# A 1-core transformer block: value products of the second batch moved from the setup into the lead of attention, and two operand stacks where there were three

## What is computed

```python
mod = jax.nn.silu(c) @ w_adaln + b_adaln
sh_msa, sc_msa, g_msa, sh_mlp, sc_mlp, g_mlp = jnp.split(mod, 6, axis=-1)
h = _modulate(_ln(x), sh_msa, sc_msa)
qkv = (h @ w_qkv + b_qkv).reshape(B, N, 3, nh, hd).transpose(2, 0, 3, 1, 4)
q, k, v = (qkv[0], qkv[1], qkv[2])
attn = jax.nn.softmax(jnp.einsum('bhqd,bhkd->bhqk', q, k) * hd ** (-0.5), axis=-1)
o = jnp.einsum('bhqk,bhkd->bhqd', attn, v).transpose(0, 2, 1, 3).reshape(B, N, C)
o = o @ w_proj + b_proj
x = x + g_msa[:, None, :] * o
...
moe = jnp.einsum('te,etc->tc', cw, eo).reshape(B, N, C)
return x + g_mlp[:, None, :] * moe
```

## Time and profile before

| | |
|---|---|
| median of three runs | 910.09 us |
| the profiled execution | 907.13 us |
| its span, first to last instruction | 905.4 us |
| PE busy in the span | 808.3 us, 89% |
| DVE, ACT, POOL busy | 568.2, 467.1, 306.4 us |
| setup, until attention begins | 73.5 us |
| lead, until the first score | 73.56 to 105.98 us |

### The profile page before, as it was taken

How to read it: one execution, slowest core, us unless ns; L and a number is a source line. 1 busy time by engine, 2 the same in 40 slices (tenths; PEclk the granted TensorE clock), 3 DMA queues, 4 the chain that set the end, 5 groups by cost and what they waited for, 6 DMA issues and landing times. The chain is left out here.

```text
span 905.4 us, 15109 instructions
## 1 busy us (share of the span) xinstructions
PE 808.3 (89%) x5083; PEld 541.6 (60%) x5083; DVE 568.2 (63%) x994; ACT 467.1 (52%) x963; POOL 306.4 (34%) x291
## 2 busy tenths in 40 slices
PE   3899899999999999999988963589999999999995
PEld 2685333333334333333323752489999999999994
DVE  3766988887787888888860985444555344343442
ACT  1360277776676777777777564243434333333431
POOL 4753200001201101000922393365455353443432
PEclk9899999999999999999999985599999999999998
DMA  9011301323130121303212882253232222222211
GB/s 255 3 33 48 76 5 26 94 76 78 23 85 20 42 63 24 77 15 79 80 54 80 248 282 90 72 143 64 55 61 45 41 38 41 47 34 45 39 32 20
DMA packets 49235, 61.82 MB, mean 68 GB/s; under 512 B 16708, under 2 KB 43186, under 8 KB 48660
## 3 DMA queue, kind: packets, MB, share of 16 engines
q1 hardware_dynamic: 39688, 46.38, 18.5%
q0 software_dynamic: 8400, 12.12, 7.8%
q10 hardware_dynamic: 1076, 2.36, 1.0%
HBM read 32.73 MB, written 15.46 MB: 53 GB/s over the span
## 5 line engine op out<-in xcount | busy, mean ns | idle before, releaser
L1102 DVE TENSOR_REDUCE negmax<-m_ps 128x2 f32<-128x1024 f32 x256 | 305.9, 1220 | 52.4 <-PE m_ps L1171 51.9
L1070 ACT ACTIVATE probs<-s_ps 128x512 f32<-128x512 f32 x495 | 260.4, 606 | 101.7 <-PE s_ps L1208 101.7
L1208 PE MATMUL s_ps<-stack 56*128 56x512 f32 x495 | 159.4, 471 | 19.3 <-ACT probs L1070 17.4
L1208 PEld LDWEIGHTS s_ps<-stack 56*128 56x128 f32 x495 | 65.3, 184 | 172.3 <-ACT probs L1070 147.7
L1222 PE MATMUL o_ps<-probs,v_aug 128*19 128x512 f32 x1024 | 134.9, 599 | 5.6 <-ACT o_sb L1077 4.6
L1171 PE MATMUL m_ps<-stack 54*128 54x512 f32 x512 | 135.5, 438 | 3.7 <-DVE o_norm L1130 1.8
L2071 PE MATMUL gate_bank<-weights,ht_hi 128*128 x630 | 127.1, 296 | 0.4 <-DVE ht_lo L1967 0.4
L2047 PE MATMUL h_ps<-weights,xt_hi 128*128 x525 | 115.2, 350 | 5.0 <-DVE xt_hi L1960 5.0
L1793 ACT CAST ht_hi<-ht_ps 128x384 fp32r<-128x384 f32 x105 | 43.5, 488 | 119.7 <-PE ht_ps L2058 119.7
L1745 POOL DMA_INDIRECT out<-res,ido x35 | 56.9, 1627 | 140.8 <-DVE res L1989 140.8
L2071 PEld LDWEIGHTS gate_bank<-weights,ht_hi 128*128 128x128 f32 x630 | 101.5, 189 | 0.6 <-issue 0.6
(11 more groups left out here) (217 smaller groups left out, 1067.7 us busy)
## 6 DMA issues: line engine op xcount, KB each, us to landing
stack<-parts SPq DMA_DIRECT2D x72, 144.0 KB
w_raw<-in_L_cond_w SPq DMA_DIRECT2D x9, 432.0 KB, 3.5
w_raw<-in_L_cond_w SPq DMA_DIRECT2D x9, 384.0 KB, 3.5
xn_scratch<-h SPq DMA_DIRECT2D x16, 192.0 KB, 4.2
x_in<-in_x SPq DMA_DIRECT2D x4, 576.0 KB, 10.1
o_scratch<-o_norm SPq DMA_DIRECT2D x16, 144.0 KB, 2.4
o_in<-o_scratch SPq DMA_DIRECT2D x16, 144.0 KB, 2.7
xr<-in_x SPq DMA_DIRECT2D x16, 144.0 KB, 3.1
```

The costliest lines, as they stand in the source:

```text
L1070: nc.scalar.activation(probs[:, st % 2, h], score_bank(k), ACT.Exp, scale=SCALE)\
L1102: nc.vector.tensor_reduce(negmax[:, half, first:first + count], m_ps[n % 2][:], AX.X, ALU.max, negate=True)\
L1208: nc.tensor.matmul(score_bank(k), stack[s][r, j, 1, kt // QT, (kt % QT) * P:(kt % QT + 1) * P], stack[s][r, j, 0, half], start=True, stop= ...
```

## The change

1. Setup makes the value products of tiles 0 to 7 alone. Those of tiles 8 to 15 (batch 1) stand in the lead, behind items 13, 14, 15, 17 to 21 (VALUES_AT), in the three `s_ps` banks that the projections use. ACT copies each into `v_aug`, POOL adds the bias. Weights and bias of the values are kept beyond the setup for that.
2. The lead's four projection units stand in thirds (2, 2 and 3 matmuls) behind items 1 to 12. All unread matmuls of the lead's items go, and of the eight ahead of it three are left. The eight at the end of setup stay.
3. STACKS goes from 3 to 2. `load_stack(g + 1)` stands at the start of SP's iteration g, and waits for the last score of group g - 1.
4. Stack 0's four heads are issued by ACT within the setup's round 18 (head 1), by SP at the setup's end (head 0), and in attention by SP (head 2) and ACT (head 3). ACT issues the four `rows_lo` transfers of the first half of group 0, SP the four `rows_hi`; ACT's stand behind its six of stack 1 and ahead of its copies of values 3 to 7.
5. The last four splits of the projection weights (L419) go from POOL's end of setup to its start of attention. POOL's fill of the third stack goes.
6. UNITS_IN: units 10 to 13 go from steps 1, 4, 7, 10 of group 2 to steps 7, 9, 11, 14; units 18 and 19 from 7, 10 to 8, 11 of group 4.

```diff
-UNITS_IN = {0: {7: 8, 10: 9}, 2: {1: 10, 4: 11, 7: 12, 10: 13}, 3: {1: 14, 4: 15, 7: 16, 10: 17}, 4: {7: 18, 10: 19}}
+LEAD_SLOTS = LEAD_UNITS + KT
+UNITS_IN = {0: {7: 8, 10: 9}, 2: {7: 10, 9: 11, 11: 12, 14: 13}, 3: {1: 14, 4: 15, 7: 16, 10: 17}, 4: {8: 18, 11: 19}}
...
-    STACKS = 3
+    STACKS = 2
...
-            heads.load_stack(sp, 0, (0, 2))
+            heads.load_stack(sp, 0, (0,))
...
             rounds((2, add_shift), extra=first_group)
-            pool.wait_ge(h_ok, NT)
-            pool.wait_ge(heads.parts_ok, SETUP_UNITS)
-            for i in (1, 2):
-                split_set(pool, wqk, heads.wqk_raw, i, (2, 3), 4 + 2 * (i + 1))
...
+                if r == STACK_AT:
+                    heads.load_stack(act, 0, (1,))
 
             rounds((5, high_part), (3, remainder), (0, normalise), extra=first_group)
-            heads.load_stack(act, 0, (1, 3))
...
             def values(t):
+                if t >= KT:
+                    return
                 pe.wait_ge(lo_ok, t + 1)
...
+VALUES_AT = (13, 14, 15, 17, 18, 19, 20, 21)
+VALUES_BESIDE_MAXIMA = 3
...
-            load_rows_of_max(0, 0)
+            heads.load_stack(sp, 0, (2,))
+            load_rows_of_max(sp, 0, 0, (0,))
             heads.load_stack(sp, 1, (2, 3))
             for g in range(GG):
+                if 1 <= g < GG - 1:
+                    load_stack(g + 1)
                 if g >= 1:
                     store(g - 1, 1)
...
                 if g + 1 < GG:
-                    load_rows_of_max(g + 1, 0)
-                if g + 2 < GG:
-                    load_stack(g + 2)
+                    load_rows_of_max(sp, g + 1, 0)
...
+            for i in (1, 2):
+                split_set(nc.gpsimd, wqk, heads.wqk_raw, i, (2, 3), 4 + 2 * (i + 1))
             heads.ones_rows(pool, 1)
             late.clear_bias_rows(nc.gpsimd)
             for n in range(SETUP_UNITS, SETUP_UNITS + LEAD_UNITS):
                 parts(n)
-            heads.ones_rows(pool, 2)
+            for i in range(KT):
+                value_bias(i)
...
+            heads.load_stack(act, 0, (3,))
             for n in range(SETUP_UNITS, SETUP_UNITS + LEAD_UNITS):
                 project(n)
+            for i in range(VALUES_BESIDE_MAXIMA):
+                value(i)
             heads.load_stack(act, 1, (0, 1))
+            load_rows_of_max(act, 0, 0, (1,))
+            for i in range(VALUES_BESIDE_MAXIMA, KT):
+                value(i)
...
+            def value(i):
+                k, t = LEAD_UNITS + i, KT + i
+                pe.wait_ge(slot_free, k + 1)
+                for n, (xs, xk, ws, wk) in enumerate(PRODUCTS):
+                    mm = nc.tensor.matmul(s_ps[k % S_BANKS][:, 0:C], heads.x[xs][:, xk, t * P:(t + 1) * P],
+                                          (wv_hi, wv_lo)[ws][:, wk], start=(n == 0), stop=(n == 6))
+                mm.then_inc(slot_mm, 1)
...
-            busy(0, 8)
+            busy(0, 3)
             for i, it in enumerate(plan.lead):
                 item(*it)
-                if i >= 4 + 2 * LEAD_UNITS:
-                    if i == 4 + 2 * LEAD_UNITS:
-                        pe.wait_ge(slot_free, S_BANKS + 2)
-                    busy(1, 2)
-                if 3 <= i < 3 + 2 * LEAD_UNITS:
-                    unit, second = divmod(i - 3, 2)
-                    project(SETUP_UNITS + unit, slice(4, len(PRODUCTS)) if second else slice(0, 4))
+                if 1 <= i < 1 + 3 * LEAD_UNITS:
+                    unit, third = divmod(i - 1, 3)
+                    project(SETUP_UNITS + unit, slice(*((0, 2), (2, 4), (4, len(PRODUCTS)))[third]))
+                elif i in VALUES_AT:
+                    value(VALUES_AT.index(i))
```

More of the change, by code:

```diff
@@ L158, in build_kernel @@
                 setup(nc, sb, pb, sem, xt, cond, w_adaln, b_adaln, w_qkv, b_qkv, x_hi, x_lo, mod_late, g_mlp, ident,
-                      half_neg, v_aug, wqk, heads, outputs_in.tiles)
+                      half_neg, v_aug, wqk, wv, heads, outputs_in.tiles)
                 late.projection_weights(far, before_experts, heads)
-                attention(nc, sb, pb, sem, w_qkv, ident, v_aug, wqk, heads, o_dram, late, outputs_in, mod_late)
+                attention(nc, sb, pb, sem, w_qkv, ident, v_aug, wqk, wv, heads, o_dram, late, outputs_in, mod_late)
             gate_bank = pb(outer, "gate_bank", [P, 512])
@@ L850, in score_item @@
     before = sum(GH * STEPS + len(UNITS_IN.get(i, ())) for i in range(g))
-    return LEAD_UNITS + before + GH * st + h + sum(st > at for at in UNITS_IN.get(g, ()))
+    return LEAD_SLOTS + before + GH * st + h + sum(st > at for at in UNITS_IN.get(g, ()))
 def proj_item(n):
@@ L899, in turn, with attention @@
         self.count += 1
-def attention(nc, sb, pb, sem, w_qkv, ident, v_aug, wqk, heads, o_dram, late, outputs_in, mod_late):
+def attention(nc, sb, pb, sem, w_qkv, ident, v_aug, wqk, wv, heads, o_dram, late, outputs_in, mod_late):
     ctx = ExitStack()
@@ L912, in attention @@
         w_split, parts_ok, stack_ld = wqk[4], heads.parts_ok, heads.stack_ld
-        heads.stacks.append(sb(ctx, "stack2", [P, 2, 2, 2, HALF], F32R))
+        wv_hi, wv_lo, bv, v_bias_ok = wv
         stack = heads.stacks
@@ L952, in score_bank, with load_rows_of_max @@
             return s_ps[k % S_BANKS][:] if k < plan.tail else (first + spare)[(k - plan.tail) % TAIL_BANKS]
+        def load_rows_of_max(eng, g, half, some=(0, 1)):
+            eng.wait_ge(max_free, 2 + plan.rows_at[2 * g + half] + 1)
+            for j in range(PAIRS):
+                for part in some:
+                    for hh in range(2):
+                        row = hh * heads.BLOCK + heads.MAX_ROW + part
+                        r = slice((hh * PAIRS + j) * QT, (hh * PAIRS + j + 1) * QT)
+                        eng.dma_start(f32(stack[g % heads.STACKS][row:row + 1, j, 0, half])
+                                      .rearrange("a (t n) -> a t n", t=QT),
+                                      f32((rows_hi, rows_lo)[part][r]))\
+                           .then_inc(rows_ld[half][j], 16)
         block = ctx.enter_context(nc.Block())
@@ L961, in load_stack @@
                 heads.load_stack(sp, g)
[L963 to L974, removed]
             def store(g, half):
@@ L1028, in parts, with value_bias @@
                 pool.wait_ge(parts_ok, heads.parts_count(n))
+            def value_bias(i):
+                to = v_aug[:, KT + i, :, 0:HD]
+                pool.wait_ge(slot_free, S_BANKS + LEAD_UNITS + i + 1)
+                nc.gpsimd.tensor_tensor(to, to, bv[:].rearrange("p (h d) -> p h d", d=HD), ALU.add).then_inc(v_bias_ok, 1)
             def stack_loaded(g):
@@ L1220, in values @@
                 tile = (g // NG) * KT + kt
+                if tile >= KT:
+                    pe.wait_ge(v_bias_ok, kt + 1)
                 for h in range(GH):
```

21 lines of the change are left out of this document (14 added, 7 removed).

## The result

The changed kernel takes 920.56 us (median of 9 runs, 917.83 to 921.73), the kernel before 910.39 beside it (9 runs, 906.1 to 916.67). The ratio is 1.0096, 95% interval 1.0068 to 1.0125: it is slower by about 1%. The profiled execution took 920.56 us, with a span of 918.6 against 905.4.

The account below looks back on a forecast made before the run. TensorE, busy 89% of the 905.4 us span, was taken as the bound, so only changes to its list or waits count. Terms -5.8 + 5.0 - 1.35 + 0.4 = -1.75 us from 910.09 gave 908.3 us; range 903.0 to 913.0.

Parts of the forecast that it names:

- Term a: End of setup: without eight value products attention begins earlier, near 67.8 us; -5.8 us, bounds -6.2 to -4.9.
- A setup that ends past 69: End of setup: a sign, listed beforehand, that the prediction is wrong; attention was expected near 67.8 us.
- Term b: Lead, start of attention to first score: it grows to 37.4 us from 32.4; +5.0 us, bounds +1.2 to +11.3.
- A to value 2: Lead, from attention's start (A) until value 2 is ready: 22.1 us, bounds 21 to 24.5, including 1.2 for low clock.
- ACT's queue: Lead: ten issues (7.5 and 2.9 us) and a 0.5 us copy delay value 6 to A+33.0; TensorE idles some 5 us.
- The rest: Lead, value 6 to first score: value 6, item 21, value 7, item 22, partly at low clock; 4.4 us.
- Term c: Groups: moving unit 10 to step 7 removes the `proj_f` wait and stall; -1.35 us, bounds -1.05 to -1.6.
- Two stacks at nothing: Groups: SP's wait for the previous group's last score is free; at most 1 us each in groups 2 and 6.
- Term d: Group 0's first steps: a low clock reaches into them where TensorE is the bound; +0.4 us, bounds 0 to 1.5.
- Rival 2: Lead: ACT's queue decides, slower than before, low clock for all that follows; +2.8 us, 912.9 us, chance 0.25.
- Rival 3: Groups: rows of maxima or stacks come late in six groups, 1.5 us each; +7 us, 917 us, chance 0.04.
- Rival 1: Lead: the clock holds and ACT's queue is cheap; sum about -5.5 us, 904.6 us, chance 0.22.

Follow-up runs that it names:

- c2: Changed kernel with the lead's projection units in halves behind items 3 to 10 instead of thirds; median 914.46 us, ratio 1.0018.
- c3: Changed kernel with ACT's ten transfers of the lead issued by SP, all rows first, then stack 1; median 910.11 us, ratio 0.9979.
- d4: Changed kernel with eight instead of three unread matmuls ahead of item 0; median 911.47 us, ratio 0.9978.
- e4: Changed kernel with one more unread matmul behind each of the twelve thirds; median 914.03 us, ratio 0.9985.
- c1: Changed kernel with 28 instead of 8 unread matmuls at the end of setup; median 908.43 us, ratio 0.9961.
- c4: Kernel before with only the new UNITS_IN steps of groups 2 and 4; median 910.37 us, ratio 0.9983.
- d3: Kernel before with two stacks instead of three, its load left where it was; median 912.65 us, ratio 0.9991.
- e1: Changed kernel with 28 unread matmuls at setup's end and all the lead's row and stack 1 transfers on SP, timed again; 899.78 us, ratio 0.9842.

## Why the prediction was wrong, step by step

**The whole.** Forecast -1.75 us and 908.3; measured +10.2 between the medians, +13.2 between the two profiled spans, and 920.56 us, outside 903.0 to 913.0. The term that failed is b, and in it one step: what the low clock costs between the start of attention and value 2. The range was also narrower than its own bounds: the upper ends of terms a to d add up to +6.85, and with the 2 us allowed for stacks to +8.85, 916.9 and 918.9 us; even these don't reach the result.

**Term a, -5.8, measured -2.84.** The mechanism was right: TensorE was no longer last, ACT's three issues ahead of two high parts set the end. Their size was not. I bounded an issue by 0.91 and 1.33 us, from rows in which six were issued in a train; these three took 5.67 us, 1.89 each. Attention began at 70.72, outside my 67.4 to 68.7. I took the trace's dearest row for an upper bound, and it wasn't one. Nor does that row show what I read in it, six issues "while SP issues too": ACT's six ran from 64.55 to 72.54, and SP's had ended at 67.23. Five traces with this setup (the changed kernel, c2, c3, d4, e4) give 5.5 to 5.7 us for the three, so the price stands. The moment at which attention begins varies by more: 68.06 to 70.72 in these five, 70.79 to 73.56 in the three with the old setup. By their means the term is -2.6. A setup that ends past 69 stood among the signs of being wrong, and it came.

**Term b, +5.0, measured +19.5** (the lead took 51.92 us against 32.42). By its own steps:

- *A to value 2: 22.1, measured 34.45.* This is the error, 12.35 us. (The steps named add up to 21.35 for the reduction of item 15, not 21.2, which is nothing beside it.) I wrote that TensorE would idle more than before ahead of the lead, and that a stretch at the low clock was likely, and then priced it by the 2.7 us that such a stretch had cost at most in the kernel before. That price belonged to a lead with eight unread matmuls ahead, halves, and unread matmuls behind later items. The change took all of these away but three. My own count of TensorE's work, "4.3 x 0.25 = 1.1 us, just under DVE's 1.18", holds at the high clock alone. At the low one it is twice that, TensorE becomes the pace, and the items come at 1.87 or more. In c1, where the clock was held, value 2 was ready at A+20.57, 1.5 before my number. The 2.7 us were also those of one execution: c4's trace of the same lead lost 5.2 us more.
- *ACT's queue: 10.9 to the start of value 6, measured 12.2.* The mechanism was right and decides: ten issues back to back, TensorE idle for 6.41 us. Of its two prices, six of the stack took 5.84, not 7.5; four of the rows took 5.83, not 2.9, above my upper bound of 4.4.
- *The rest: 4.4, measured 5.27,* with the clock fallen in the idle stretch, as forecast.

In c1, then, the first score came at A+37.30 against A+37.4 in the sum. That they agree to 0.1 is luck, since value 2 came 1.5 us early, and the queue (11.76 against 10.9) and the rest (4.97 against 4.4) took as much more. But the sum was that of a lead whose clock stays up until ACT's queue, and this was the unstated condition of all its terms.

**Term c, -1.35, measured -1.85** in group 2 (104.99 us against 106.84 from rows to rows), and -1.89 alone in c4. "Units 18 and 19: nothing" was wrong by 0.6 us. Two stacks at nothing: right, by d3.

**Term d, +0.4:** from the first score to the next rows the distance grows from 16.66 to 16.94, so 0.3.

**The rivals.** Rival 2 named the right second cause, at 0.25, and put the point of decision at a first score of 106.5; it came at 122.64. But even its price, 912.9, fell short, for it too took A+22.1 for value 2. No rival had the lead itself at the low clock. Rival 3 didn't happen. Rival 1 is refuted as told, since in the kernel as it is the clock falls twice; c1 restores its first condition up to ACT's queue, and c3 takes the queue away, worth 12.1 and 10.5 us of the median.

**The Trainium skill.** The Trainium skill (TensorE: Matmul & The Clock Gate, Part 1) says that idleness throttles and activity releases. The trace agrees on the falls at 69.1 and 113.5, both in idle stretches. On the release it agrees only in part: with TensorE busy at 1.00 in the records, 35 us did not release it, while with five more unread matmuls it was released at 74.7 (d4). I had used the rule against rival 1 alone, at ACT's queue, where it was right, and not at the setup's end, where the greater idle stretch lay in my own sum (65.5 to A). The other rule is that of the Trainium skill (DMA: Bandwidth & Descriptors, "Issuing engines are not separate DMA queues"): transfers from several engines run on the same 16 DMA engines. That an issue is therefore dearer beside another queue was my own conclusion, and the traces don't bear it out: ACT's six of the stack took 5.84 us while SP issued its rows, against 6.28 alone. It was the rows that were dear, so that the sum of the ten, 11.7 us against 10.4, came near by two errors that partly cancel.

## What to carry to other kernels

When a change takes filler or dense work from the matrix engine, work out its longest idle stretch ahead of each paced stretch, and price the paced stretch at both clocks in full: not by what a low stretch cost while the filler was there. If the engine falls to the low clock and then becomes the pace itself, the loss lasts as long as the stretch, and a few matmuls ahead of it, placed where the wait really is, are a cheap cure: five of them took 9 us off here (d4). And read the lead of more than one execution before pricing a low stretch by it. Don't let an engine issue transfers ahead of compute that others wait for; at 1.0 to 1.9 us an issue, ten of them held ACT for 10.2 to 11.8 us.

## What the chip showed that I had not expected

- The granted clock stayed at 0.50 from 69.1 to 106.6 us, the last 35 us of it under a TensorE that reads as busy without a gap. It rose in the fourth value product. What brings the rise stays open.
- With the clock at 1.00 at the start, the same stream of thirds held it at 1.00 (c1, d4, e1). In these traces the clock at the beginning of such a stretch was the clock of the whole of it. The unread matmuls in the later lead of the kernel before did no better: one execution of that code ran them at 1.00, another at 0.50 from 98.1 us on (c4), with the same idle stretch of 1.41 us shortly before in both.
- An issue of a stack's transfer cost ACT 0.97 to 1.0 us in a train of six in the lead and 1.82 to 1.89 in the three at setup's end; one of the small row transfers cost 1.05 to 1.46 on ACT in the lead, where two of them took SP 1.19 (0.60 each) in the groups. What sets the price of an issue, no run here shows.
- The kernel before ranges from 905.83 to 921.23 us, and its mean granted clock goes with it, from 0.962 to 0.94. The version with both cures ran nine times of ten between 898.29 and 901.3, at 0.955 to 0.964, and once in 912.46, at 0.944; where in the program the clock fell in that one, no trace shows.
